# Max pooling over a graph's neighbours: the features stand still in TensorE and the selection of four tiles streams past, block by block

## The reference, cut to what matters

```
h = relu(layernorm(x))
out = max(adj @ (h @ W0) + b0, 0)                        # features, 4096 x 128
pooled[i, :] = max over all j with adj[i, j] != 0 of out[j, :]
x = x + pooled
h = relu(layernorm(x));  x = x + [h, adj @ h] @ W1       # the second layer, and so on
```

## Time and profile before

| what | us |
|---|---|
| median of three runs | 1737.51 |
| lowest, highest | 1735.72, 1738.18 |
| the profiled execution, its own time | 1733.34 |
| its span from first to last instruction | 1731.3 |
| pool stage in it, first gather to last GpSimd instruction | 398.08 to 704.03 |

### The profile page before, as it was taken

How to read it: one execution, slowest core, us unless ns; L and a number is a source line. 1 busy time by engine, 2 the same in 40 slices (tenths; PEclk the granted TensorE clock), 3 DMA queues, 4 the chain that set the end, 5 groups by cost and what they waited for, 6 DMA issues and landing times.

```text
span 1731.3 us, 37002 instructions
## 1 busy us (share of the span) xinstructions
PE 1557.3 (90%) x11433; PEld 1025.4 (59%) x11433; DVE 1276.2 (74%) x3508; ACT 700.7 (40%) x1113; POOL 571.4 (33%) x792
## 2 busy tenths in 40 slices
PE   3699999978889888899998999699999999988996
PEld 3467767756677676666655666578644444445553
DVE  5499999988899999635665677532399999983454
ACT  2434444425555555123342323466556555540000
POOL 2423222337777777201110000133200000017776
PEclk9999999988999999999999999899999999999998
DMA  4477777743343333222213322244200000005553
GB/s 159 163 269 272 287 263 294 278 170 91 105 121 104 112 102 114 83 97 93 89 61 97 97 85 88 77 121 128 85 1 7 6 6 6 6 19 166 168 163 86
DMA packets 97579, 205.12 MB, mean 118 GB/s; under 512 B 10912, under 2 KB 61728, under 8 KB 89328
## 3 DMA queue, kind: packets, MB, share of 16 engines
q1 hardware_dynamic: 73008, 172.58, 29.0%
q0 software_dynamic: 11840, 25.52, 5.3%
q10 hardware_dynamic: 12672, 6.29, 1.2%
HBM read 178.13 MB, written 26.21 MB: 118 GB/s over the span
## 4 chain that ended last, share of the span: by engine, by line
PE 49%; DVE 22%; issue 15%; POOL 7%; DMA 3%; ACT 2%; DVEq 1%; POOLq 1%; SPq 1%; ACTq 0%
PE bank L688 17%; PE bank L557 7%; PE bank L756 6%; DVE partsA L2085 6%; POOL gath L1391 4%; PE bank L642 4%; PE bank L823 4%; PE bank L562 2%; PE bank L542 2%; DVE gath L1681 2%; DVE cand L1548 2%; PE bank L522 2%; DMA gath<-last_features,IDX 2%; PE bank L586 1%; PE bank L512 1%
## 5 line engine op out<-in xcount | busy, mean ns | idle before, releaser
L688 PE MATMUL bank<-partsB,panel 128*128 128x387 bf16 (+1 forms) x2048 | 350.3, 332 | 16.5 <-POOL partsB L1181 8.7
L688 PEld LDWEIGHTS bank<-partsB,panel 128*128 128x128 fp8e4 x2048 | 201.8, 99 | 160.8 <-issue 12.7
L823 PE MATMUL bank<-wide,partsA 128*128 128x512 f32 x512 | 263.2, 596 | 6.4 <-ACT rows L1105 4.9
L642 PE MATMUL bank<-partsB,first 128*128 128x128 bf16 x3072 | 222.9, 222 | 38.0 <-DVE gath L1681 21.6
L1548 DVE MAX8 cand<-bank 128x8 f32<-128x128 f32 x1024 | 216.7, 279 | 39.4 <-POOL found L1214 19.9
L642 PEld LDWEIGHTS bank<-partsB,first 128*128 128x128 fp8e4 x3072 | 195.4, 99 | 83.0 <-issue 64.8
L557 PE MATMUL bank<-partsA,panel 128*128 128x387 bf16 x1024 | 216.5, 334 | 22.6 <-DVE cand L1548 15.1
L890 ACT ACTIVATE panel<-bank 128x1024 fp8e4<-128x1024 bf16 x128 | 130.7, 1023 | 172.9 <-PE bank L542 172.9
L1303 POOL DMA_INDIRECT gath<-pool_features,idx_now x160 | 162.8, 1017 | 55.2 <-issue 46.6
L1105 ACT COPY rows<-bank 128x512 f32<-128x512 f32 x256 | 133.3, 615 | 116.3 <-DVE partsA L2101 87.6
L1681 DVE TENSOR_REDUCE gath<-bank 128x128 f32<-128x512 f32 x256 | 173.1, 681 | 8.6 <-PE bank L642 8.1
(11 more groups left out here) (274 smaller groups left out, 2099.6 us busy)
## 6 DMA issues: line engine op xcount, KB each, us to landing
rows<-in_adj SPq DMA_DIRECT2D x64, 1024.0 KB, 7.2
panel<-adjT_panels SPq DMA_DIRECT2D x128, 512.0 KB
adjT_panels<-panel SPq DMA_DIRECT2D x32, 512.0 KB, 3.0
panel<-adjT_panels SPq DMA_DIRECT2D x64, 256.0 KB, 2.9
gath<-pool_features,idx_now POOLq DMA_INDIRECT x160
overflow_maxima<-wide POOLq DMA_DIRECT2D x1, 2048.0 KB, 17.4
pool_features<-gsc ACTq DMA_DIRECT2D x8, 256.0 KB, 2.3
rows<-overflow_maxima SPq DMA_DIRECT2D x8, 256.0 KB
```

The lines of the kernel that those rows point to most:

```text
L642: i = pe.matmul(first_bank(n, peeled)[:, b * P:(b + 1) * P], first[:, q % 2, j, :], pparts[:, j, k * FE:k * FE + F], start=(k == 0), stop= ...
L688: i = pe.matmul(bank[q][:, 0:3 * w], panel[:, q, j, :], of_block if w < FE else parts_of[u][:, j, :], start=(j == 0), stop=(j == NT - 1))
L823: pe.matmul(o[:, :], zs[:, q % 2, :], zT[:, c * 512:(c + 1) * 512], start=True, stop=False)
```

## The change

The two operands of the selection product change places. The feature part of one source block is now stationary (128 x 128 bf16) and the selections of that block for all four tiles of the group move past it, 512 columns at once (`select`, in place of TensorE's `firsts`). The result of a block is 128 features x (4 tiles x 128 rows). So VectorE no longer reduces inside a chunk: it keeps two running maxima of 128 x 512 over the 32 blocks (`take_block`), joins them at the end of the group, and TensorE turns the joined maximum back in four transposes (`turn_firsts`), which `pool_floor` reads in a new first step.

With it change:

- the loads: one piece of 128 x (4 tiles x 512 bytes) for each four blocks of a group (`load_piece`) in place of a panel for each tile;
- `first`, which becomes a ring of 16 slots, with two PSUM banks for the triangular products, six blocks ahead (`tri_block`);
- the gather buffers, now four (`main`), one for each tile of a group, and `after_chunk` is gone; the store of the overflow maxima moves ahead of tile 3;
- `tree`, which joins only the 5 gathered rows in three steps of 256, 128 and 128 elements;
- the places of the other steps between the blocks.

The core of the diff:

```diff
-            def firsts(g, q, last, c0=0, c1=NT // BPB, peeled=False):
...
-                    for b in range(BPB):
-                        j = c * BPB + b
-                        for k in range(3):
-                            i = pe.matmul(first_bank(n, peeled)[:, b * P:(b + 1) * P], first[:, q % 2, j, :],
-                                          pparts[:, j, k * FE:k * FE + F], start=(k == 0), stop=(k == 2))
-                    i.then_inc(s_fp, 1)
+            def select(g, j):
+
+                pe.wait_ge(s_first, NT * g + j + 3)
+                pe.wait_ge(s_fp_used, NT * g + j + 1)
+                pe.sem_inc(waited["pe"], 1)
+                for k in range(3):
+                    i = pe.matmul(pool_bank[j % 4][:, :], pparts[:, j, k * FE:k * FE + F], first_slot[:, j % SLOTS, :],
+                                  start=(k == 0), stop=(k == 2))
+                i.then_inc(s_fp, 1)
...
             def pool_turn(g, first_group, last):
...
+                for j in range(NT):
+                    if first_group:
+                        if j == 8:
+                            overflow_records()
+                    else:
+                        if j == 5:
+                            turn_firsts(g - 1)
+                        if j == 25:
+                            aux_transposes(1, g - 1)
+                        if j == 28:
+                            aux_products(1, g - 1)
+                    select(g, j)
+                    if j + AHEAD < NT:
+                        tri_block(g, j + AHEAD)
...
             def gathers(g, q):
                 t = g * G + q
                 pool.wait_ge(s_idx, t + 1)
                 pool.wait_ge(s_gath_used, t + 1)
                 pool.sem_inc(waited["pool"], 1)
                 for k in range(MAIN):
-                    if k == PAUSE:
-                        after_chunk(t if q == 2 else t - 1, 1 if q == 2 else 6)
...
                     if q == 1:
                         overflow_gathers(g)
-                store_overflow(g)
+                    if q == 2:
+                        store_overflow(g)
...
-                dve.tensor_reduce(gath[:, q % 2, MAIN + c, :],
-                                  first_bank(q * (NT // BPB) + c, peeled).rearrange("p (b f) -> p f b", b=BPB),
-                                  axis=AX, op=ALU.max).then_inc(s_fp_used, 1)
+            def take_block(g, j, first_group=False):
+
+                n = NT * g + j
+                if j < 2:
...
+                    dve.tensor_copy(running[:, j, :], pool_bank[j][:, :]).then_inc(s_fp_used, 1)
+                else:
+                    dve.wait_ge(s_fp_used, n + 3)
+                    dve.wait_ge(s_fp, n + 1)
+                    dve.tensor_tensor(running[:, j % 2, :], running[:, j % 2, :], pool_bank[j % 4][:, :], ALU.max
+                                      ).then_inc(s_fp_used, 1)
+                if j == NT - 1:
+                    dve.wait_ge(s_fp_used, n + 5)
+                    dve.tensor_tensor(firsts_all[:, :], running[:, 0, :], running[:, 1, :], ALU.max
+                                      ).then_inc(s_firsts_all, 1)
...
             def turn(g, peeled, second=False, last=False):
...
+                for j in range(NT):
+                    take_block(g, j, peeled)
+                    if not (peeled or second):
+                        if j == 2:
+                            remainder(g - 2)
+                        if j == 25:
+                            part2(g - 2)
...
+                        if 3 <= j < 6:
+                            tree(before, G - 1, j - 3, (g, G - 1))
+                        if 6 <= j < 9:
+                            pool_floor(before, j - 6)
+                        if 9 <= j < 11:
+                            pool_post(before, j - 9)
+                        if 14 <= j < 16:
+                            pool_post(before, j - 12)
+                        if j == 16:
+                            pool_post(before, 5)
+                        if j == 20:
+                            pool_post(before, 4)
+                        if j == 30:
+                            operand(1, g - 1)
+                    elif j == 12:
+                        overflow_indices()
+                    for q, j0 in ((0, 11), (1, 17), (2, 26)):
+                        if j0 <= j < j0 + 3:
+                            tree(g, q, j - j0, None if last else (g + 1, q))
+                    if 21 <= j < 25:
+                        overflow_maxima(g, j - 21)
```

More of the change, by code:

```diff
@@ L1582, in _ @@
             dve.wait_ge(s_list_idx, ISTEPS_OF_LIST * NG)
-            for q in range(2):
+            for q in range(G):
                 dve.tensor_copy(idx_now[:, q, :], IDX[:, q, 0:MAIN]).then_inc(s_idx, 1)
@@ L1779, in turn @@
                 before = 0 if second else g - 1
-                def at(q, c):
-                    take_firsts(g, q, c, peeled and q < 2, peeled)
-                at(0, 0)
-                if not (peeled or second):
-                    remainder(g - 2)
-                for c in range(1, 5):
-                    at(0, c)
-                    if not peeled:
-                        tree(before, G - 1, c - 1, (g, 1))
-                at(0, 5)
-                for c in range(6, 8):
-                    at(0, c)
-                    if not peeled:
-                        pool_floor(before, c - 6)
@@ L1796, in turn @@
-                if peeled:
-                    overflow_indices()
-                at(1, 0)
-                if not peeled:
-                    pool_post(before, 0)
-                for c in range(1, 5):
-                    at(1, c)
-                    tree(g, 0, c - 1, (g, 2))
-                if not (peeled or second):
-                    part2(g - 2)
-                for c in range(5, 8):
-                    at(1, c)
-                    if not peeled:
-                        pool_post(before, c - 4)
@@ L1812, in turn @@
-                at(2, 0)
-                if not peeled:
-                    pool_post(before, 4)
-                for c in range(1, 5):
-                    at(2, c)
-                    tree(g, 1, c - 1, (g, 3))
-                for c in range(5, 8):
-                    at(2, c)
-                    overflow_maxima(g, c - 5)
-                at(3, 0)
-                overflow_maxima(g, 3)
-                at(3, 1)
-                tree(g, 2, 0)
-                at(3, 2)
-                if not peeled:
-                    operand(1, g - 1, aux_bank[1])
@@ L1828, in turn @@
-                for c in range(3, 6):
-                    at(3, c)
-                    tree(g, 2, c - 2, None if last else (g + 1, 0))
-                for c in range(6, 8):
-                    at(3, c)
+                for j in range(NT):
+                    take_block(g, j, peeled)
+                    if not (peeled or second):
+                        if j == 2:
+                            remainder(g - 2)
+                        if j == 25:
+                            part2(g - 2)
+                    if not peeled:
+                        if 3 <= j < 6:
[19 more added lines that the diff above has]
+                        overflow_maxima(g, j - 21)
```

245 lines of the change are left out of this document (104 added, 141 removed).

## The result

| | before | after |
|---|---|---|
| median, us | 1737.14 (4 runs) | 1723.76 (4 runs) |
| lowest, highest | 1735.72, 1738.18 | 1722.49, 1724.73 |
| profiled execution, and its span | 1733.34, 1731.3 | 1722.49, 1720.8 |

The ratio is 0.9922, with a 95% interval from 0.9907 to 0.9937: 13.4 us less. I had forecast 6.3 us less and a time of 1731.2. The direction held. The range (1723 to 1740) held by 0.8 us only, and its low end stood there for a rival, not for the forecast case: the gain is twice the one forecast, beyond the 1728 to 1734 of that case.

A forecast was written before the change was run, and what follows sets the result against it. GpSimd's gathers were taken to bound the stage, VectorE close behind. Terms -5.3 + 1.5 + 0.6 - 3.1 = -6.3 us took the median from 1737.5 to 1731.2; range 1723 to 1740, forecast case 1728 to 1734 (chance 0.50).

The forecast's parts named there:

- the index waits: GpSimd's five waits for indices staged by VectorE would vanish with four buffers: -5.3 us.
- The long gathers: GpSimd gathers averaging 1.017 and 1.046 us, not 0.95, 15.8 us in all, were expected to stay: no change counted.
- the removed pauses: Rival: pauses between gathers caused the long ones, so GpSimd shortens by up to 10 us more, 1721; chance 0.13.
- The first group: GpSimd's first copy of overflow indices comes late, near 414.9, because index steps stand behind block 12: +1.5 us.
- The copies: GpSimd's copy of the overflow indices would keep its 0.98 us behind it: no change.
- The stores: GpSimd's store ahead of tile 3 would not wait for overflow maxima, with 1.5 us of cover in each group.
- the rival: Late landing or takes use up the store's cover; 0.8 us a group cancels the gain: 1734 to 1741, chance 0.23.
- the 0.76 from which VectorE would decide: Rival: VectorE's takes step at 0.76 us or more, not 0.61, and bound the stage; 1758 at 0.86; chance 0.14 with clock.
- TensorE: right: TensorE's block would cost 0.84 us against 0.91 a chunk; the saving lies beside GpSimd and is worth nothing.
- The clock: Rival: TensorE pauses once a group and its clock falls to 1.2 GHz: +51 us, 1788; chance 0.14 with VectorE as bound.
- the -3.1 of that term: At the stage's end TensorE starts the second layer 1.6 us before GpSimd's end, not 1.5 behind: -3.1 us.
- The other chain: Tile 3's rows, tree, floor and layer norm end at 710.6, before TensorE's transposes at 711.1: 0.5 us of cover.

The follow-up runs named there:

- Experiments 1 and 2: Changed kernel plus a 768-element VectorE operation beside each tree, with two SBUF inputs (1984.38 us, ratio 1.0261) or one (1985.61 us, 1.0264).
- experiment 3: Changed kernel with the pauses' waits and counting instructions put back between the gathers: 1973.99 us, ratio 1.0216 to the kernel before.

## Why the prediction was right, and where its size was off

**The bound, and the index waits: right, by the first chip's traces.** There the stage is GpSimd's work almost without a stop, before and after, and its end moved with it; 5.3 us of waits are gone and 0.30 stands before each gather, as forecast. On the other chips GpSimd is not the bound.

**The long gathers: the step that failed.** "The gathers' mean is 1.017 and 1.046 us, not the usual 0.95 (...) I leave them, since they stand at branches and loop ends, which stay." They do not stand there. They stand under VectorE's two-input operations, which the change makes shorter and fewer. Over all 221 DMAs, the excess over 0.95 was about 16.1 us and is 8.4: a term of -7.7 us that I set to nothing. Experiments 1 and 2 show the mechanism; that it is the removed pauses, which I gave a chance of 0.13 and up to 10 us, experiment 3 excludes. That the measured time still fell within the stated range, by 0.8 us, is luck as far as this term goes: the low end was held open for that wrong cause.

**The first group.** The copy was forecast at 414.9 and stands at 415.25: +1.9 us for +1.5. **The copies.** I kept the 0.98 behind each; it is 0.81 now, -1.4 us in eight. By experiment 3 this part is the removed pause. **The stores.** Forecast without a wait; two of eight wait 0.8 us each, +1.0 over the usual gap. The cover of 1.5 us was nearly used: the rival was close, but it came to no more than this.

**GpSimd's sum**, by its measured terms: -5.3 - 7.7 - 1.4 + 1.9 + 1.0 = -11.5 us, against 305.9 - 294.5 = 11.4.

**VectorE: right.** Takes follow each other at 0.60 us (681.27 to 681.87 below) and last 677 ns in the mean, not the 0.76 from which VectorE would decide. Its waits for rows I had growing from 2 to about 5 us a group. They are 27.5 / 8 = 3.4, and the 2 was misread: it holds the waits for chunks too, those for rows alone were 8.3 / 8 = 1.0. **TensorE: right.** A block takes 0.86 us (404.04 to 404.90), forecast 0.84.

```profile
404.04 0.38 PE L586 MATMUL bank<-panel,tri 128*128 128x512 fp8e4 x1
404.25 0.81 PE L615 MATMUL bank<-first,partsB 128*128 128x512 fp8e4 x3
404.90 0.38 PE L586 MATMUL bank<-panel,tri 128*128 128x512 fp8e4 x1
```

**The clock: a rival in small.** A granted clock below 0.95 stood on my list of what would show the prediction wrong, and it came: 0.91 in one of the windows above, after TensorE had stood still for 5.4 us up to 568.1 (0.96 in the one before, after 2.5 us up to 497.5). So the sign was badly chosen, for the stage does not feel those two, as I had written for a clock that falls only behind the pause; but in the last group it does. VectorE in order of time:

```profile
680.49 0.86 DVE L1695 TENSOR_TENSOR gath<-gath 128x640 f32<-128x640 f32 x1 [5.04 <-DMA gath<-pool_features,rest]
681.27 0.67 DVE L1659 TENSOR_TENSOR gath<-gath,bank 128x512 f32<-128x512 f32 x1
681.87 0.54 DVE L1698 TENSOR_TENSOR gath<-gath 128x384 f32<-128x384 f32 x1
...
688.63 0.69 DVE L1659 TENSOR_TENSOR gath<-gath,bank 128x512 f32<-128x512 f32 x1 [1.54 <-PE bank L615]
...
694.11 0.42 DVE L1677 TENSOR_TENSOR gath<-gath 128x256 f32<-128x256 f32 x1 [0.87 <-DMA gath<-pool_features,idx_now]
```

VectorE waited 5.04 us for overflow rows, TensorE stood still behind it, its clock was at 1.2 GHz from 680.6 to 687.4, its layer products took 1.60 us where eight like them take 1.06 at 706.72, and VectorE waited 1.54 for a block. So TensorE starts the second layer 0.56 us before GpSimd's end and not 1.6: -2.0 us for the -3.1 of that term. The other chain kept up, with 0.26 us (transposes at 704.37, `hn` done at 704.11) of the 0.5 forecast.

**The whole:** -11.4 - 2.0 + 0.5 = -12.9 us, against 13.0 measured at 716.04 and 13.4 (10.9 to 16.2) in the medians. With the long gathers counted the forecast would have been -6.3 - 7.7 = -14.0. The other terms that were off come to +1.1 together.

## What to carry to other kernels

A mean above the usual duration is a term of the sum: list the long ones and look at what the other engines ran when each began, before calling them part of the place. Keep VectorE's two-input operations in SBUF short while GpSimd issues gathers, or give them one operand from PSUM. And a queue that issues without a stop, once its waits are gone, may not suit every chip: here the same change gave 0.8% on one and lost 2.4% on another, and on a third the waits of two buffers brought the changed kernel level with the kernel before.

## What the runs showed of the hardware that was not expected

- A gather started under a VectorE operation with both inputs in SBUF ends 0.82 to 0.86 us after that operation, be it 0.41 or 4.45 us long (3.86 us for a gather of 0.95). An operation with one input from PSUM (0 of 68 gathers), or a reduction of 768 elements in SBUF (0 of 12), holds none.
- On some chips takes run at 2.0 to 4.0 us each while gathers are issued and at 1.2 to 1.4 while they are not, with waits of up to 16 us without a releaser in the trace; in the stretch shown they end with late semaphore updates of TensorE. Between 100 and 300 us of the span, with no gather there, the chips are alike (the windows 100 to 200 and 200 to 300 differ by at most 0.4 us of TensorE's busy time). The cause stays open.
- The granted clock was at 1.2 GHz from 571.4 to 578.2 us, after TensorE had stood still for 5.4 us, and from 499.7 to 503.1, after 2.5 us; it stayed at 2.4 GHz after 2.9 us up to 460.9. What decides it, no run here shows.
